# Global attention as a three-tile pipeline across batches, with the layer 0 weights split inside it

## What is computed

```python
mod = (silu(c) @ wmod).reshape(4, 6, 1, 128)       # sa, ca, ga, sb, cb, gb
ga, gb = sign(ga) * max(|ga|, 0.25), sign(gb) * max(|gb|, 0.25)
h = layernorm(x) * (1 + ca) + sa                   # the first norm
q, k, v = h @ Wq + bq, h @ Wk + bk, h @ Wv + bv
x = x + ga * softmax(q @ k.T / sqrt(128)) @ v      # global attention, 1024 x 1024 a batch
h = layernorm(x) * (1 + cb) + sb                   # the second norm
for i in range(6):                                 # local layers, 16 heads of 64, windows of 32
    h = local_attention(shift(h), Wqkv[i], ...) @ Wo[i] + h
    h = gated_ffn(shift(h), ln_g[i], ln_b[i], W1[i], b1[i], W2[i], b2[i]) + h
return x + gb * h
```

## Time and profile before

| | us |
|---|---|
| median of 3 runs | 3696.93 (3695.18 to 3698.4) |
| the profiled execution's own time | 3698.82 |
| its span, first to last instruction | 3697.0 |
| up to the first local projection (L736) | 326.35 |
| first scores of batch 0, and of batch 3 | 37.60, 259.00 |
| TensorE busy, share of the span | 93% |
| mean granted TensorE clock | 0.975 |

### The profile page before, as it was taken

How to read it: one execution, slowest core, us unless ns; L and a number is a source line. 1 busy time by engine, 2 the same in 40 slices (tenths; PEclk the granted TensorE clock), 3 DMA queues, 4 the chain that set the end, 5 groups by cost and what they waited for, 6 DMA issues and landing times.

```text
span 3697.0 us, 132440 instructions
## 1 busy us (share of the span) xinstructions
PE 3426.7 (93%) x50548; PEld 2640.8 (71%) x50548; DVE 2640.4 (71%) x5823; ACT 2508.1 (68%) x5117; POOL 2356.0 (64%) x1568
## 2 busy tenths in 40 slices
PE   5666999999999999999999999999999999999997
PEld 4444877777777777777777777777777777777774
DVE  3445877777877777877777877777877777877773
ACT  2224766677777777777777776777776777777774
POOL 1004866667767667767667766667766667767662
PEclk9888999999999999999999999999999999999998
DMA  2000111121111121111121111121111121111111
GB/s 79 0 0 12 48 37 44 37 63 41 50 36 44 39 61 43 47 36 44 41 59 44 47 36 44 39 61 43 47 36 44 41 59 44 47 36 44 41 39 44
DMA packets 98169, 156.71 MB, mean 42 GB/s; under 512 B 18129, under 2 KB 39633, under 8 KB 96721
## 3 DMA queue, kind: packets, MB, share of 16 engines
q1 hardware_dynamic: 93440, 132.73, 13.3%
q10 hardware_dynamic: 4176, 15.74, 1.3%
HBM read 20.48 MB, written 2.10 MB: 6 GB/s over the span
## 4 chain that ended last, share of the span: by engine, by line
PE 77%; issue 6%; ACT 5%; POOL 1%; DVE 1%; ACTq 0%; DMA 0%; DVEq 0%; POOLq 0%; SPq 0%
PE psum L736 19%; PE psum L760 11%; PE psum L826 9%; PE psum L846 7%; PE psum L783 6%; PE psum L803 4%; PE psum L791 4%; PE psum L866 4%; PE psum L878 3%; PE psum L871 3%; PE psum L755 2%; PE psum L857 1%; PE psum L853 1%; ACT probT L553 1%; ACT aoT L510 1%
## 5 line engine op out<-in xcount | busy, mean ns | idle before, releaser
L377 POOL TENSOR_TENSOR qkr<-qks,rnorm 128x1024 f32<-128x1024 f32 x384 | 731.3, 1904 | 371.0 <-issue 291.1
L369 POOL TENSOR_TENSOR qks<-work 128x1024 f32<-128x1024 f32 x384 | 908.0, 2365 | 72.1 <-DVE work L1042 67.8
L385 POOL TENSOR_TENSOR probn<-prob,psumr 128x512 f32<-128x512 f32 x384 | 400.5, 1043 | 506.4 <-DVE psumr L1068 506.4
L536 ACT ACTIVATE sq<-psum 128x512 f32<-128x512 f32 x768 | 463.9, 604 | 346.9 <-PE psum L736 346.3
L736 PE MATMUL psum<-whi,xhi 128*128 128x512 f32 x1152 | 565.1, 491 | 107.0 <-issue 67.2
L1016 DVE TENSOR_REDUCE ssq<-sq 128x8 f32<-128x512 f32 x768 | 515.6, 679 | 48.6 <-ACT sq L536 12.2
L1040 DVE TENSOR_TENSOR work<-psum,rot 128x512 f32<-128x512 f32 x768 | 507.4, 661 | 58.6 <-POOL qks L369 43.3
L1074 DVE TENSOR_REDUCE nmax<-psum 128x8 f32<-128x512 f32 x384 | 264.9, 690 | 335.9 <-PE psum L760 334.6
L760 PEld LDWEIGHTS psum<-kT,qbd 128*64 128x64 f32 x12288 | 403.8, 142 | 109.9 <-issue 109.9
L760 PE MATMUL psum<-kT,qbd 128*64 128x64 f32 x12288 | 458.6, 230 | 0.9 <-issue 0.8
L736 PE MATMUL psum<-whi,xlo 128*128 128x512 f32 x1152 | 458.7, 398 | 0.0
(11 more groups left out here) (131 smaller groups left out, 6490.3 us busy)
## 6 DMA issues: line engine op xcount, KB each, us to landing
vsh<-vtok SPq DMA_DIRECT2D x384, 192.0 KB, 2.5
vsh<-vtok SPq DMA_DIRECT2D x384, 64.0 KB, 3.1
xsh<-xs_in SPq DMA_DIRECT2D x192, 64.0 KB, 2.0
ff_x<-x_mid SPq DMA_DIRECT2D x96, 128.0 KB
wqkv<-Wqkv_dram ACTq DMA_DIRECT2D x5, 1536.0 KB, 7.7
wo_next<-Wo_dram ACTq DMA_DIRECT2D x5, 512.0 KB, 8.3
xtok<-x_dram SPq DMA_DIRECT2D x4, 512.0 KB, 11.0
out_dram<-qkr SPq DMA_DIRECT2D x8, 256.0 KB, 2.5
```

Source lines behind the costliest of these rows:

```text
L369: pool.tensor_tensor(qks[:, :, :], rcos, rsin, ALU.add).then_inc(s["add_ready"], 1)
L377: pool.tensor_tensor(qkr[:, j % 2, :, :], qks[:, :, :], rnorm[:, :].unsqueeze(2).to_broadcast([P, 2 * OCT, DH]), ALU.mult).then_inc(s["qkr ...
L385: pool.tensor_tensor(probn[:, :, :], prob[:, j % 2, :, :], psumr[:, j % 2, 1, :].unsqueeze(2).to_broadcast([P, OCT, KEYS]), ALU.mult).then ...
L536: act.activation(sq[:, w * OCT:(w + 1) * OCT, :], bank[w].rearrange("p (h n) -> p h n", n=DH), ACT.Square).then_inc(s[("sqq_ready", "sqk_r ...
```

## The change

The loops over the batches are written out, and the work of three tiles and of two batches is interleaved on each engine.

- TensorE runs `scores_global(i + 2)`, `turn_global(i + 1)`, `attend_global(i)`. ScalarE and VectorE follow in that order.
- In iteration 6 of a batch, TensorE turns the first norm of the next batch, and in iteration 7 it projects that batch's q (k behind tile 7, then v). VectorE takes the next batch's statistics in iterations 3 and 4 and normalises it in iteration 5.
- The second norm of a batch is taken inside the next batch: statistics at its start, normalising in iteration 1, transposes in iterations 2 and 3 through bank 7. Only the last batch's stands behind its attention.
- The first norm of batch 0 stands before the modulation chain on VectorE, with a semaphore of its own for batch 0's x (`x_first`). The clamp's scratch moves from `sq` to `sdiff` and `probn`.
- `weights_high(0, .)` runs on ScalarE in iterations 1 to 3 of batch 0, `weights_low(0, .)` on GpSimd behind the first inverse.
- SP's first local turn waits for batch 0's second norm alone (`gout_ready`); TensorE no longer waits for `pad_ready`, SP does ahead of its second turn. ScalarE issues its loads in the order c, wmod, wa.

```diff
+NORMS = ((0, 0), (1, 0), (0, 1), (2, 0), (1, 1), (3, 0), (2, 1), (3, 1))
+NORM_AT = {bw: n for n, bw in enumerate(NORMS)}
...
     SP
+                if isinstance(t.units, int) and t.units <= UNROLL:
+                    sp.wait_ge(s["gout_ready"], 2 if t.first else 2 * B)
+                    if not t.first:
+                        sp.wait_ge(s["pad_ready"], 1)
...
-            sp.wait_ge(s["gh_ready"], 4 * B)
-            sp.wait_ge(s["pad_ready"], 1)
...
     GpSimd
+            global_inverse(0)
+            for k in range(len(SECTIONS)):
+                weights_low(0, k)
+            for n in range(1, 2 * B):
+                global_inverse(n)
...
     ScalarE
+            def exponential_global(b, i):
+                n = b * TPB + i
+                act.wait_ge(s["gm_ready"], n + 1)
+                if n >= 2:
+                    act.wait_ge(s["gt_ready"], n - 1)
+                    act.wait_ge(s["gri_step"], n - 1)
...
+            normed_first(0)
+            for n in range(4):
+                projected(0, n)
+            for b in range(B):
+                exponential_global(b, 0)
+                exponential_global(b, 1)
+                turned_global(b, 0)
+                for i in range(TPB):
+                    if i + 2 < TPB:
+                        exponential_global(b, i + 2)
+                    if i == 6 and b + 1 < B:
+                        normed_first(b + 1)
+                    if i + 1 < TPB:
+                        turned_global(b, i + 1)
+                    if i in (2, 3) and b:
+                        normed_second(b - 1, i - 2)
+                    if i in (1, 2, 3) and b == 0:
+                        weights_high(0, 2 * i - 2)
+                        weights_high(0, 2 * i - 1)
+                    if i == 7 and b + 1 < B:
+                        for n in range(4):
+                            projected(b + 1, n)
+            for half in range(2):
+                normed_second(B - 1, half)
...
     TensorE
+            def turn_global(b, i):
+                n = b * TPB + i
+                pe.wait_ge(s["ge_ready"], n + 1)
+                pe.wait_ge(s["gte_a"], n)
+                pe.wait_ge(s["gte_d"], n)
...
+            def attend_global(b, i):
+                n = b * TPB + i
+                pe.wait_ge(s["gte_a"], n + 1)
+                pe.wait_ge(s["gte_d"], n + 1)
+                pe.wait_ge(s["gx_ready"], n)
+                pe.wait_ge(s["gvs_ready"], b * 2 + 2)
...
+            for half in range(2):
+                norm_turn(0, 0, half)
+            project_global(0, 0)
+            project_global(0, 1)
+            project_values(0)
+            for b in range(B):
+                scores_global(b, 0)
+                scores_global(b, 1)
+                turn_global(b, 0)
                 for i in range(TPB):
+                    if i + 2 < TPB:
+                        scores_global(b, i + 2)
+                    if i == 6 and b + 1 < B:
+                        for half in range(2):
+                            norm_turn(b + 1, 0, half)
                     if i + 1 < TPB:
-                        scores(i + 1)
-                    turn(i)
-                    values(i)
-                for half in range(2):
-                    norm_turn(b * 2 + 1, half)
+                        turn_global(b, i + 1)
+                    if i == 7 and b + 1 < B:
+                        project_global(b + 1, 0)
+                    attend_global(b, i)
+                    if i in (2, 3) and b:
+                        norm_turn(b - 1, 1, i - 2)
+                if b + 1 < B:
+                    project_global(b + 1, 1)
+                    project_values(b + 1)
+            for half in range(2):
+                norm_turn(B - 1, 1, half)
...
     VectorE
+            dve.wait_ge(s["x_first"], 16)
+            global_stats(0, 0, TPB)
...
+            global_normed(0)
...
+            values_global(0)
+            for b in range(B):
+                row_max(b, 0)
+                row_max(b, 1)
+                if b:
+                    dve.wait_ge(s["gx_ready"], b * TPB)
+                    global_stats(b - 1, 0, TPB // 2)
+                turned_global(b, 0)
+                if b:
+                    global_stats(b - 1, TPB // 2, TPB)
                 for i in range(TPB):
+                    inverse_global(b, i)
+                    if i + 2 < TPB:
+                        row_max(b, i + 2)
+                    updated(b, i)
                     if i + 1 < TPB:
+                        turned_global(b, i + 1)
+                    if i == 1 and b:
+                        global_normed(b - 1)
+                    if i in (3, 4) and b + 1 < B:
+                        if b == 0 and i == 3:
+                            dve.wait_ge(s["x_in"], 16 * (B - 1))
+                        global_stats(b + 1, (i - 3) * 4, (i - 2) * 4)
+                    if i == 5 and b + 1 < B:
+                        global_normed(b + 1)
+                if b + 1 < B:
+                    values_global(b + 1)
+            dve.wait_ge(s["gx_ready"], B * TPB)
+            global_stats(B - 1, 0, TPB)
+            global_normed(B - 1)
```

More of the change, by code:

```diff
@@ L647, in attention @@
                 sweep(act, body)
-            for k in range(len(SECTIONS)):
-                weights_high(0, k)
             act.wait_ge(s["const_in"], 16 * 2)
@@ L692, in _ @@
                     mm.then_inc(s["gv_ready"], 1)
-                for n in range(4):
-                    pe.wait_ge(s["gqk_ready"], b * 4 + n + 1)
-                def scores(i):
-                    if i >= 2:
-                        pe.wait_ge(s["ge_ready"], b * TPB + i - 1)
-                    for half in range(2):
-                        mm = pe.matmul(bank[i % 2 * 2 + half], qT[:, i * P:(i + 1) * P], kgT[:, half * 512:half * 512 + 512],
-                                       start=True, stop=True)
-                    mm.then_inc(s["gs_ready"], 1)
@@ L725, in _, with scores_global @@
-                scores(0)
-                for i in range(TPB):
-                    if i + 1 < TPB:
-                        scores(i + 1)
-                    turn(i)
-                    values(i)
-                for half in range(2):
-                    norm_turn(b * 2 + 1, half)
+            def scores_global(b, i):
+                n = b * TPB + i
+                pe.wait_ge(s["gqk_ready"], b * 4 + 4)
+                if n >= 2:
+                    pe.wait_ge(s["ge_ready"], n - 1)
+                for half in range(2):
+                    mm = pe.matmul(bank[i % 2 * 2 + half], qT[:, i * P:(i + 1) * P], kgT[:, half * 512:half * 512 + 512],
+                                   start=True, stop=True)
+                mm.then_inc(s["gs_ready"], 1)
@@ new lines, in turned_global, with inverse_global @@
+            def turned_global(b, i):
+                n = b * TPB + i
+                dve.wait_ge(s["gt_ready"], n + 1)
+                dve.wait_ge(s["go_ready"], n)
+                dve.tensor_copy(pgT[:, 4:8, :], bank[5].rearrange("p (a n) -> p a n", a=4)).then_inc(s["gte_d"], 1)
+            def inverse_global(b, i):
+                n = b * TPB + i
+                dve.wait_ge(s["ge_ready"], n + 1)
+                if n >= 2:
+                    dve.wait_ge(s["gx_ready"], n - 1)
+                dve.reciprocal(gsum[:, i % 2, 1:2], gsum[:, i % 2, 0:1]).then_inc(s["gri_step"], 1)
```

202 lines of the change are left out of this document (96 added, 106 removed).

## The result

The changed kernel takes 3658.08 us (3655.41 to 3662.62) against 3697.66 before, a ratio of 0.9895 [0.9877, 0.9912]. That is 39.6 us faster; 91.6 were forecast, and 3658 lies above the range of 3595 to 3625.

What follows compares the result with a forecast made beforehand. In the first 326 us a closed ring of 5.91 us a tile and serial batch boundaries were taken to bound the kernel; 6.94 + 77.6 + 6.8 + 6.3 - 6.0 = 91.6 us saved gave 3605.3, range 3595 to 3625.

Steps and rivals of the forecast that it cites:

- from there on the same 3370 us as before: Sign in the changed profile: from the first local projection (near 235 us) on, the local layers take unchanged time.
- Slower: Rival, 48 local loop bodies: moved code stalls fetching; 1.9 us each cancels the gain, 3 us gives 3749; chance 0.02.
- start: Before batch 0's first scores: normalising ahead of the modulation chain brings them from 37.60 to 30.66, saving 6.94 us.
- three batches, before any clock loss: First scores of batch 0 to those of batch 3: 143.8 us instead of 221.4, saving 77.6.
- clock at three boundaries: TensorE may fall to 1.2 GHz after idling between batches: 2.0 us lost at each, minus 6.0, bounds 0 and 9.
- last batch, to the end of its values: Batch 3's global attention: 41.3 us instead of 48.07, saving 6.8.
- weights and tail to the first projection: Weight splitting moves from behind the last norm to tiles 1 to 3 of batch 0: 2.8 instead of 9.1, saving 6.3.
- Tile: Global attention's tile loop: with three tiles in flight TensorE sets the period, 4.51 us instead of 5.91.
- A new wait inside the tile: Rival, global tile loop: unseen handoffs hold the period at 5.0 to 5.5 us, giving 3620 to 3635; chance 0.13.
- The pipeline does nothing: Rival, global tile loop: the single buffer keeps 5.91 us a tile, 39 us not won, giving 3644; chance 0.05.
- The stall before the norm's transposes: Iteration 6 of a batch: TensorE idles 3.56 us until VectorE has normalised the next batch, turn(7) queued behind.
- Low clock through the boundary: Rival, between batches: lowered clock stays until the next scores, costing 18 us instead of 6, giving 3617; chance 0.13.

Runs made afterwards that it cites:

- pe108_after: Changed kernel with 54 one-column matmuls (108 instructions) that do nothing but move code, at the start of TensorE's program: 3604.73 us, ratio 0.9727.
- pe148_before: Kernel before the change with 74 one-column matmuls (148 instructions) at the start of TensorE's program: 3759.0 us, ratio 1.0145.
- flat_all: Changed kernel with the inner loops over blocks 2 to 6 and the loop over the layers written out: 3480.34 us, ratio 0.9404.
- flat_order: Changed kernel, inner loops written out, with turn(7) and the values of tile 6 ahead of the next norm's transposes: 3491.88 us, ratio 0.9444.
- flat_weights_back: Changed kernel, inner loops written out, with the splitting of the weights moved back behind the last norm: 3508.15 us.
- pe256_after: Changed kernel with 128 one-column matmuls (256 instructions, a whole 16384-byte block) at the start of TensorE's program: 3658.07 us.
- pe40_after: Changed kernel with 20 one-column matmuls (40 instructions) at the start of TensorE's program: 3626.13 us.

## Why the prediction was wrong

**The step that failed** is the last one of the profile to come: "from there on the same 3370 us as before". It measured 3428.1. The mechanism was among the rivals, as *Slower*, with a chance of 0.02: unrolling moves where each later loop body starts, and a fetch stall in each body takes the gain back. In its place the runs showed this: at each of the 28 returns TensorE stands still, with fetches of code under way, and behind most of them it works for some us at 1.2 GHz; both depend on where the loop heads lie, and with the heads as the change left them the layers had 25.0 us more idle and 32.5 us more busy time. The kernel did not end on that rival's side, since the price was 57.5 / 48 = 1.2 us a body and not the 1.9 that it needed, or 2.1 for each of the 28 returns. pe108_after and pe148_before show it from both sides: the same shift of TensorE's heads gives 49 us of span to one kernel and takes 63 from the other.

**The argument that misled** was "a busy share of 93% leaves no sign of a stall". The rest of the span is 3697.0 - 3426.7 = 270 us, 148 of them in the local layers, where TensorE stood still "<- issue" for 67.2 us, 24 times, at the line that opens the bodies. Besides, the share counts a matmul at the low clock as busy, and 36 us of that lay in the layers already (3222.73 against 3186.49 in flat_all). I had read the first 326 us closely and the rest by its busy share. Asked for its waits, the trace would have shown stalls of up to 3.8 us at the returns, whose size nothing held in place.

**The rule on fetching.** The Trainium skill (Runtime: NRT & Kernel Launch, section "Instruction fetch mechanics") says that code is fetched in blocks of 16 KiB and that a taken branch whose target is not at hand waits for a fetch. The traces agree: fetches of 16384 bytes, no stall in the written-out code of flat_all, a taken branch of 3.3 to 5.4 us at each return before and after. The prediction cited it and drew only that the unrolled part gains; the returns that were there already it did not ask after.

**The terms of the sum**, by the same points of the timeline:

| term | forecast | measured |
|---|---|---|
| start, first scores 37.60 to 30.04 | 6.94 | 7.6 |
| three batches, before any clock loss | 77.6 | 82.1 |
| clock at three boundaries | -6.0 | -5.8 |
| last batch, to the end of its values | 6.8 | 7.9 |
| weights and tail to the first projection | 6.3 | 6.8 |
| local layers | 0 | -57.5 |

The first five sum to 98.6 against 91.6, the six to 41.1, the difference of the spans.

- *Start*: right. TensorE's first matmul came 0.54 us earlier because the loads landed earlier, which is most of the 0.6 beyond the forecast.
- *Tile*: TensorE sets the period, as said; it is 4.38 and not 4.51, since values and transposes issue in 1.78 and 0.88 rather than the 1.86 and 0.93 that I read from rows of a tile with gaps. A batch gains by that 5 x 0.13 = 0.65 in its full periods, 0.21 before them and 0.28 behind the stall, and 0.23 in the stall itself: 1.37. Batches 1 and 2 gain 0.2 more each, since the 0.15 for a delayed maximum did not appear. Together that is the 4.5 that the batches have beyond their term. The rivals *A new wait inside the tile* and *The pipeline does nothing* did not happen: behind a batch's first turn, and while scores are left to issue, no row of TensorE in a tile has a bracket.
- *The stall before the norm's transposes*: 3.33 us from the end of the values' issue (3.16 of them idle) where 3.56 stood, in all three boundaries, released by VectorE's normalising as written.
- *Clock*: transposes, turn and values behind the stall would take 0.93 + 0.88 + 1.78 = 3.59 us at the full rate, and took 4.91, 6.43 and 5.24: 1.32, 2.84 and 1.65 lost. The windows after the change show the granted clock at 0.50, that is 1.2 GHz, behind the stall (column before the last two):

```profile
96.00:108.00 12.00, 12.00 (x77) 1.00 0.05 11
...
114.00:119.00 5.00, 5.00 (x25) 0.50 0.00 0
```

  (3.12 us for the sixteen values at 116.78 instead of 1.95, for one.) It was back before the next batch's scores, whose eight records take 3.60 us in each batch, so the rival *Low clock through the boundary* did not happen. flat_order shows that the idle stretch is what costs it: with 1.20 us instead of 3.16 the clock stays at 1.00.
- *Weights*: 6.8 by the table and 7.5 by flat_weights_back, where 6.3 stood. The six subtractions beside the tiles:

```profile
45.89 2.51 POOL L359 TENSOR_TENSOR wlo<-wqkv,whi 128x512 fp32r<-128x512 f32 x2 [34.77 <-ACT whi L512]
```

  1.25 us each against 7.37 / 6 = 1.23 alone, with the tile's period at 4.38 there as elsewhere. The Trainium skill (SBUF — State Buffer, section "Who interferes with whom") would have GpSimd and an instruction of VectorE in a two-port mode or with two SBUF inputs lock each other out. Here no such cost can be seen; but VectorE's larger rows beside the subtractions are maxima, copies and updates that read the PSUM, and statistics that read one tile, so that this is no test of the rule.

**A slip in the forecast.** The first scores near 31, 78, 128 and 178 do not follow from its own terms, which give 31, 80, 130 and 180 with the clock's loss. Measured were 30.04, 77.20, 126.74 and 175.10.

**What stays open.** Which rule inside a block makes a head dear. The table maps thirteen places, each in one loop; it does not say why the second stall comes for heads near 100 to 140, and TensorE's records may miss register instructions, so that the numbers are distances from each other and not addresses (the layer loop's may lie some five records further on). Why the low clock lasts longer behind the returns of the changed kernel is open too. That a body's own alignment or the end of the loop plays a part was not tested apart from the head, since every pad moves both.

## What to carry to other kernels

Before an edit that changes the length of an engine's code ahead of a loop, ask the trace for "<- issue" at the first line of the loop bodies, and for the granted clock behind it: what stands there is paid at each return, and its size changes with the placement by several us, in either direction. A comparison of two versions is fair only when the loop heads of the busiest engine lie alike or the loops are written out; here a pad of 108 instructions was worth more than the pipeline's whole visible gain. Where the program allows it, writing the loops out takes the cost away altogether: 3658 us became 3480, 178 off where the pipeline itself gives 99.

## What the runs showed of the hardware that was not expected

- A return to a loop head costs 2.8 to 9.8 us of a body of 66.0, in a kernel whose bodies hold about 2145 TensorE records, and it repeats with a period of 256 instructions: pe256_after has the bodies of the kernel without the pad within 0.2 us.
- More than half of what a bad placement cost was busy time, not idle time: 32.5 of 57.5 us, with the granted clock at 0.50 for 196 us of the local layers instead of 114.
- TensorE's taken branch itself took 3.6 to 5.2 us on average, by loop and placement, and the branch that is not taken 0.08. A second stall, of up to 3.6 us in pe40_after, can follow inside the scores, close behind the body's start.
- The other engines pay at a return as well (2.91 us on VectorE, 4.35 on ScalarE in the return shown), yet lengthening their streams gave nothing back (its median was 12 us higher, unexplained), and moving TensorE's heads did.
- Written out as a whole, 129,378 instructions run without such a stall in the bodies, at 3245.5 us from the first projection to the last matmul against 3365.3 before.
